# Row scores and causal mask of an attention step, written in squares of 32 output rows

## The chip, the core and the metric

The kernel runs on one core of a Trainium2 chip. The metric is the device time of one execution in microseconds (us), as the median of several runs. Before the change it is 2014.7 us, the median of 3 runs that lie between 2012.65 and 2017.67 us.

## What is computed

64 images of 3 x 224 x 224 are cut into 196 patches each and projected to 256 features; a bias and a position table are added, and 32 text rows are appended, so that a sequence has 228 rows. One transformer layer follows:

```python
h = _L0_tok_ref(x, W_embed, b_embed, pos_embed)
h = jnp.concatenate([h, txt], axis=1)                 # 64 x 228 x 256
h = h + attention(_layernorm(h), Wq, Wk, Wv, Wo, bo)   # 16 heads of 16, causal
h = h + ffn(_layernorm(h), w_up, w_down)               # ternary weights, 1024 wide, gelu
...
scores = jnp.einsum('bhqd,bhkd->bhqk', q, k) / jnp.sqrt(jnp.float32(hd))
scores = jnp.where(causal, -jnp.inf, scores)
probs = jax.nn.softmax(scores, axis=-1)
```

## The kernel before

Two sequences make a pair (32 pairs). A sequence is held as two blocks of R = 114 rows. The program is a software pipeline written out by hand: `step(t, hs)` has eight sections k = 0 to 7, and in step t it works on four pairs at once, pair t (patches, embedding, normalisation, queries and keys), pair t-1 (row scores and values), pair t-2 (column scores, softmax, weighted values) and pair t-3 (projection and feed-forward). There are 35 steps. The order of the work on each engine is the order of the calls in its own `step`; waits on semaphores tie the engines together.

The softmax needs the largest score of every query row. For that the scores are computed twice:

- **Row scores** (`scores_rows`, line 495): queries on the partitions, keys along the free axis. Section k takes one sequence of the pair and four heads. VectorE takes the maximum along the rows (`maxima_unit`, lines 951 and 952) and the maxima are folded into the queries. Only the maxima of these scores are used.
- **Column scores** (`scores_columns`, line 475): keys on the partitions. ScalarE takes their exponential (line 674), GpSimd zeroes what is above the diagonal (line 1155), and TensorE multiplies with the values (`weighted_values`, into the tile `pvps`).

In `scores_rows` four heads are worked on side by side. Head i has its queries and keys on the 32 partitions `quad(i)`, so that its matmul uses one strip of 32 rows of the array, and it writes to a PSUM bank of its own, `score[:, i]`. For query block qb = 0 a head has one matmul with 114 output rows and 114 keys, for qb = 1 one with 114 output rows and 228 keys. Both operands are float32; such a matmul stands in the trace as two loads and two matmuls, called its two passes below. Then the causal mask is added, in bfloat16: `cmask` holds a large negative number above a diagonal, `idm` a 32 x 32 identity with zeros to its left and right. For j = 0 to 3 a matmul per head adds the mask to output rows 32j and up of both diagonal blocks. All of its 114 output rows are written; those that aren't of piece j get zeros from the zeros around the identity. One call of `scores_rows` thus has 8 float32 matmuls (16 in the trace) and 16 bfloat16 ones, and it is made 8 times for each pair, 256 times in all. It is called the **row unit** below. Its last matmul signals VectorE.

Around a row unit in section k stand matmuls that use the whole array and write to the tile `dense` (embedding, up and down projection and so on), then the column scores (the tile `score`, `km` as the stationary operand), then the weighted values. A column unit has 8 float32 matmuls, and so has a unit of the weighted values; its squares are strips of 32 output rows over all rows of the array.

All matmuls pass through one helper, line 324, so that the trace's groups on it are told apart by their tiles: `score<-km,qm` are row scores, `score<-cmask,idm` the mask, `score<-qm,km` column scores, `pvps<-pr,vp` weighted values.

Of the kernel before, what the change touches and what calls it, by code (L numbers as in the profile page):

```python
# [39 lines left out]
S = NPATCH + TXT  # L40
R = S // 2
# [11 lines left out]
SW = S + R  # L53
# [22 lines left out]
def build(nc, x, txt, w_embed, b_embed, pos, wqkvo, bo, w_upT, w_downT, out):  # L76
    with ExitStack() as ctx:
        def sb(name, shape, dt):
            return ctx.enter_context(nc.sbuf_tensor(name, shape, dt))

        def sem(name):
            return ctx.enter_context(nc.semaphore(name))
# [3 lines left out]
        idm = sb("idm", [128, R + 96], BF16)  # L86
        cmask = sb("cmask", [128, R + 96], BF16)
# [21 lines left out]
        qm = sb("qm", [128, 2, 2, 2, T2], F32)  # L109
        km = sb("km", [128, 2, 2, 2, T2], F32)  # L110
# [42 lines left out]
        score = ctx.enter_context(nc.psum_tensor("score", [128, 4, 512], F32))  # L153
# [19 lines left out]
        p = {n: sem("p_" + n) for n in ["mask", "gl", "bo", "rstd1", "pw2", "acc", "ss", "w"]}  # L173
# [5 lines left out]
        def count(per, pair, k):  # L179


            return (min(pair, NPAIR - 1) if isinstance(pair, int) else pair) * per + k
# [34 lines left out]
        def score_emptied(t, k, columns):  # L217

            m, back = 2 * k + (1 if columns else 0) - 1, 0
            while back < 3:  # L220
                if m < 0:
                    m, back = m + 16, back + 1
                if m % 2 == 1:
                    pair, q = columns_of(t - back, m // 2)
                    if live(pair):
                        return a["exp"], count(8, pair, q + 1)
                elif live(t - back - 1):
                    return v["max"], count(8, t - back - 1, m // 2 + 1)
                m -= 1
            return a["w"], 1  # L230
# [91 lines left out]
        def _(eng):  # L322
            def mm(*args, **kw):
                return nc.tensor.matmul(*args, **kw)  # L324
# [147 lines left out]
            def quad(i):  # L472
                return slice(32 * i, 32 * i + 32)
# [21 lines left out]
            def scores_rows(t, u, k):  # L495

                b, r = divmod(k, 4)
                m, par = divmod(r, 2)
                if b == 0:
                    eng.wait_ge(a["q"], count(4, t - 1, 2 * m + par + 1))  # L500
                    if par == 0:
                        eng.wait_ge(v["km"], count(2, t - 1, m + 1))
                    else:
                        eng.wait_ge(a["km"], count(2, t - 1, m + 1))

                eng.wait_ge(*score_emptied(t, k, False))
                for qb in range(2):
                    for i in range(4):
                        mm(score[0:R, i, qb * R:qb * S + R], qm[quad(i), par, 1 - u, m, b * S + qb * R:b * S + qb * R + R],
                           km[quad(i), 1 - u, m, par, b * S:b * S + R + qb * R], start=True, stop=False,  # L510
                           skip_group_check=True)
                for j in range(4):
                    for i in range(4):
                        o = score[0:R, i, 0:SW].rearrange("p (x w) -> p x w", w=R)[:, 0:3:2, 32 * j:R]
                        above = cmask[quad(i), 96:96 + R - 32 * j].rearrange("p (o w) -> p o w", o=1)
                        last = mm(o, idm[quad(i), 96 - 32 * j:96 - 32 * j + R], above.broadcast_to([32, 2, R - 32 * j]),
                                  start=False, stop=True, skip_group_check=True)
                last.then_inc(pe["s"], 1)

# [35 lines left out]
            def step(t, hs):  # L555
                u = hs % 2
                A, Bm, Cc, Dd = live(t), live(t - 1), live(t - 2), live(t - 3)
                for k in range(8):
                    if Bm:
                        scores_rows(t, u, k)  # L560
# [695 lines left out]
```

## Time and profile before

| | |
|---|---|
| median of 3 runs | 2014.7 us |
| the profiled execution's own time | 2019.13 us |
| its span, first to last instruction | 2017.4 us |
| TensorE busy | 1927.3 us (96%), 25090 matmuls |
| VectorE busy | 1465.9 us (73%) |
| ScalarE busy | 1312.9 us (65%) |
| GpSimd busy | 892.5 us (44%) |
| granted TensorE clock, mean | 0.978 of full speed |

The times of a single instruction in the trace overlap with those of the next ones, since matmuls are pipelined: a matmul's record reaches from its issue to a modelled end. What a unit costs is read from where the next unit starts. In the timeline, rows of equal operation and tiles are merged into one, with the first one's shapes and the number of them; a narrow window lists those alone that are under way in it.

### The profile page before, as it was taken

The page shows a single profiled execution, that of the slowest core. Times are in us where ns is not written, and L with a number is a line of the kernel's source. Part 1 is how long each engine was busy: PE and PEld are TensorE (multiplying, and loading weights), DVE is VectorE, ACT ScalarE, POOL GpSimd, SP SyncE. Part 2 cuts the span into 40 slices and gives each one's busy share as a digit, 9 for nine tenths or more (in the row PEclk, how much of TensorE's full clock was granted, in tenths as well). Part 3 has the DMA queues.
Part 4 walks back from the last instruction along what each step waited for, and adds up shares of the span by engine and source line. Part 5 has one row for each costly group of instructions (what it writes and reads, how often), then busy time and mean ns, then how long its engine had stood idle before and what let it go on. Part 6 is the DMA issues. An engine that isn't in the chain of part 4 may idle for free.

```text
span 2017.4 us, 59822 instructions
## 1 busy us (share of the span) xinstructions
PE 1927.3 (96%) x25090; PEld 1574.9 (78%) x25090; DVE 1465.9 (73%) x2717; ACT 1312.9 (65%) x1986; POOL 892.5 (44%) x1067
## 2 busy tenths in 40 slices
PE   4779999999999999999999999999999999999975
PEld 3668888888888888788888888888888888888754
DVE  3667778777777777777777777777777778777753
ACT  3347766666776676767667677666667766667652
POOL 1124444444444544444454444444454445444543
PEclk8789999999999999999999999999999999999987
DMA  5011111111111101111111111111111111010000
GB/s 149 15 46 41 50 55 50 35 45 44 53 50 55 50 27 53 41 55 50 53 47 31 47 49 51 54 50 35 45 45 52 50 55 50 30 51 17 30 29 24
DMA packets 66116, 93.72 MB, mean 46 GB/s; under 512 B 10082, under 2 KB 59718, under 8 KB 65592
## 3 DMA queue, kind: packets, MB, share of 16 engines
q1 hardware_dynamic: 65848, 89.90, 15.6%
q8 instruction: 199, 3.26, 0.7%
q14 instruction: 69, 0.57, 0.1%
HBM read 45.03 MB, written 14.94 MB: 30 GB/s over the span
## 4 chain that ended last, share of the span: by engine, by line
PE 90%; ACT 3%; DVE 3%; issue 2%; POOL 1%; DMA 1%; SPq 0%; DVEq 0%; POOLq 0%; ACTq 0%
PE dense L324 50%; PE score L324 21%; PE pvps L324 9%; PE dense L342 4%; PE dense L381 3%; ACT qm L699 2%; PE dense L552 2%; PE dense L370 1%; POOL acc L1174 1%; DMA borow<-bo 1%; DVE mx L952 1%; ACT pr L674 0%; DVE st L936 0%; DVE mx L951 0%; ACT xn L723 0%
## 5 line engine op out<-in xcount | busy, mean ns | idle before, releaser
L1155 POOL TENSOR_SCALAR_AFFINE_SELECT pr<-pr 114x456 f32<-114x456 f32 x512 | 310.8, 631 | 853.2 <-ACT pr L674 853.2
L674 ACT ACTIVATE pr<-score 114x1368 f32<-114x1368 f32 x256 | 335.6, 1311 | 301.3 <-PE score L324 301.0
L951 DVE TENSOR_REDUCE mx<-score 114x4 f32<-114x456 f32 x256 | 161.1, 629 | 260.3 <-PE score L324 259.7
L952 DVE TENSOR_REDUCE mx<-score 114x4 f32<-114x912 f32 x256 | 281.0, 1098 | 0.0
L324 PE MATMUL dense<-wdn,g 128*114 128x256 bf16 x1024 | 243.4, 283 | 2.0 <-ACT g L683 1.2
L324 PE MATMUL score<-qm,km 32*114 32x228 f32 (+1 forms) x4096 | 221.8, 331 | 18.7 <-DVE mx L952 15.4
L324 PE MATMUL dense<-wdn,gl 128*114 128x256 bf16 x1024 | 236.6, 276 | 0.0
L1174 POOL TENSOR_TENSOR acc<-acc,sq 128x456 f32<-128x456 f32 x192 | 222.4, 1158 | 19.0 <-POOL acc L1174 0.4
L324 PEld LDWEIGHTS score<-qm,km 32*114 32x114 f32 x4096 | 176.0, 175 | 69.4 <-issue 40.5
L324 PE MATMUL score<-km,qm 32*114 32x114 f32 (+1 forms) x4096 | 221.8, 331 | 7.5 <-ACT pr L674 6.7
L324 PE MATMUL pvps<-pr,vp 114*32 114x228 f32 (+1 forms) x4096 | 205.2, 318 | 1.0 <-ACT raw L741 0.6
L908 DVE RECIPROCAL rs<-rs 128x228 f32<-128x228 f32 x128 | 200.5, 1566 | 5.5 <-DMA cx<-raw 5.5
L324 PEld LDWEIGHTS score<-km,qm 32*114 32x114 f32 x4096 | 127.1, 175 | 60.1 <-issue 37.9
L324 PEld LDWEIGHTS pvps<-pr,vp 114*32 114x32 f32 x4096 | 108.5, 110 | 68.9 <-POOL pr L1155 10.9
L683 ACT ACTIVATE g<-dense 128x456 f32<-128x456 f32 x256 | 135.1, 553 | 29.9 <-PE dense L324 29.4
L324 PEld LDWEIGHTS dense<-wdn,g 128*114 128x114 bf16 x1024 | 137.3, 134 | 19.8 <-issue 16.3
L324 PE MATMUL dense<-pT_hi,we_hi 128*128 128x392 f32 x384 | 142.3, 371 | 3.8 <-DVE pT_lo L898 2.2
L691 ACT ACTIVATE sq<-g 128x456 f32<-128x456 f32 x256 | 142.2, 580 | 1.4 <-POOL acc L1174 1.4
L324 PE MATMUL dense<-xT_hi,wup 128*128 128x456 f16 x512 | 142.8, 361 | 0.1
L716 ACT ACTIVATE vp<-dense 114x512 f32<-114x512 f32 x64 | 41.1, 642 | 156.2 <-PE dense L324 156.2
L324 PE MATMUL dense<-xT_lo,wup 128*128 128x456 f16 x512 | 141.7, 359 | 0.0
L324 PEld LDWEIGHTS dense<-wdn,gl 128*114 128x114 f16 x1024 | 136.2, 133 | 0.0
(125 smaller groups left out, 4402.5 us busy)
## 6 DMA issues: line engine op xcount, KB each, us to landing
pix<-x SPq DMA_DIRECT2D x64, 588.0 KB
rs<-raw SPq DMA_DIRECT2D x256, 57.0 KB, 2.0
cx<-raw SPq DMA_DIRECT2D x256, 57.0 KB, 2.0
out<-h SPq DMA_DIRECT2D x64, 228.0 KB
h<-txt SPq DMA_DIRECT2D x32, 64.0 KB, 7.1
km<-wqkvo SPq DMA_DIRECT2D x1, 1024.0 KB, 13.7
h<-w_upT SPq DMA_DIRECT2D x1, 1024.0 KB, 14.1
km<-w_embed SPq DMA_DIRECT2D x1, 768.0 KB, 6.6
```

The costliest lines, as they stand in the source:

```text
L324: return nc.tensor.matmul(*args, **kw)
L342: last = nc.tensor.transpose(ps[:, i * PROWS:(i + 1) * PROWS], patches[:, ph, n], ident[0:PROWS, 0:PROWS])
L381: last = nc.tensor.transpose(ps[:, col(blk, b):col(blk, b) + R], src[:, c0:c0 + 128], ident[0:R, 0:R])
L674: act(pr[q % 2][:], score[0:R, :, 0:SW], ACT.Exp, scale=float(HD) ** -0.5).then_inc(a["exp"], 1)
L683: act(g[:, m], bank_of("up", m)[:, 0:T2], ACT.Gelu).then_inc(a["gelu"], 1)
L691: act(sq[:, m % 4], g[:, m], ACT.Square).then_inc(a["sq"], 1)
L716: act(dst, bank_of("v", k)[0:R, 0:2 * D].rearrange("p (e c) -> p e c", c=HD), ACT.Copy).then_inc(a["v0"], 1)
L908: nc.vector.reciprocal(rs[:, k % 2], rs[:, k % 2]).then_inc(v["rs"], 1)
L951: nc.vector.tensor_reduce(mx[:, m, 0, x:128:32], score[0:R, :, 0:R], AX.X, ALU.max)
L952: nc.vector.tensor_reduce(mx[:, m, 1, x:128:32], score[0:R, :, R:SW], AX.X, ALU.max).then_inc(v["max"], 1)
L1155: nc.gpsimd.affine_select(out=blocks, in_=blocks, compare_op=ALU.is_ge, fill=0.0, base=0, pattern=[[0, 4], [1, R]], channel_multiplier=-1) ...
L1174: tt(acc[:], sq[:, 0] if m == 1 else acc[:], sq[:, m % 4], ALU.add).then_inc(p["acc"], 1)
```

## The change

Each float32 matmul of 114 output rows becomes four of 32, 32, 32 and 18 output rows, with the same moving operand. Each mask matmul writes the 32 (or 18) output rows that belong to its piece j, with the identity alone as the stationary operand. Queries of rows 32j and up are loaded into rows of strip i and columns 32j to 32j+31 of the array: a square (i, j). A row unit has 32 float32 matmuls (64 in the trace) and 16 bfloat16 ones then. Nothing else is changed, on no other engine.

```diff
                 eng.wait_ge(*score_emptied(t, k, False))
                 for qb in range(2):
+                    for j in range(4):
+                        lo, hi = 32 * j, min(32 * j + 32, R)
+                        for i in range(4):
+                            mm(score[lo:hi, i, qb * R:qb * S + R],
+                               qm[quad(i), par, 1 - u, m, b * S + qb * R + lo:b * S + qb * R + hi],
+                               km[quad(i), 1 - u, m, par, b * S:b * S + R + qb * R], start=True, stop=False,
+                               skip_group_check=True)
+                for j in range(4):
+                    lo, hi = 32 * j, min(32 * j + 32, R)
                     for i in range(4):
-                        mm(score[0:R, i, qb * R:qb * S + R], qm[quad(i), par, 1 - u, m, b * S + qb * R:b * S + qb * R + R],
-                           km[quad(i), 1 - u, m, par, b * S:b * S + R + qb * R], start=True, stop=False,
-                           skip_group_check=True)
-                for j in range(4):
-                    for i in range(4):
-                        o = score[0:R, i, 0:SW].rearrange("p (x w) -> p x w", w=R)[:, 0:3:2, 32 * j:R]
-                        above = cmask[quad(i), 96:96 + R - 32 * j].rearrange("p (o w) -> p o w", o=1)
-                        last = mm(o, idm[quad(i), 96 - 32 * j:96 - 32 * j + R], above.broadcast_to([32, 2, R - 32 * j]),
+                        o = score[lo:hi, i, 0:SW].rearrange("p (x w) -> p x w", w=R)[:, 0:3:2, lo:R]
+                        above = cmask[quad(i), 96:96 + R - lo].rearrange("p (o w) -> p o w", o=1)
+                        last = mm(o, idm[quad(i), 96:96 + hi - lo], above.broadcast_to([32, 2, R - lo]),
                                   start=False, stop=True, skip_group_check=True)
                 last.then_inc(pe["s"], 1)
```

On TensorE, in section 3 between two groups of the up projection, the row unit stood in the program before as follows (output shapes are written behind the tiles; a float32 matmul is one row here).

```order
L324 MATMUL dense<-xT_hi,wup 128x456 x2
L324 MATMUL dense<-xT_lo,wup 128x456 x2
L324 MATMUL score<-km,qm 114x114 x4
L324 MATMUL score<-km,qm 114x228 x4
L324 MATMUL score<-cmask,idm 114x2x114 x4
L324 MATMUL score<-cmask,idm 114x2x82 x4
L324 MATMUL score<-cmask,idm 114x2x50 x4
L324 MATMUL score<-cmask,idm 114x2x18 x4
L324 MATMUL dense<-xT_hi,wup 128x456 x2
L324 MATMUL dense<-xT_lo,wup 128x456 x2
```

The same place in the changed program:

```order
L324 MATMUL dense<-xT_hi,wup 128x456 x2
L324 MATMUL dense<-xT_lo,wup 128x456 x2
L324 MATMUL score<-km,qm 32x114 x12
L324 MATMUL score<-km,qm 18x114 x4
L324 MATMUL score<-km,qm 32x228 x12
L324 MATMUL score<-km,qm 18x228 x4
L324 MATMUL score<-cmask,idm 32x2x114 x4
L324 MATMUL score<-cmask,idm 32x2x82 x4
L324 MATMUL score<-cmask,idm 32x2x50 x4
L324 MATMUL score<-cmask,idm 18x2x18 x4
L324 MATMUL dense<-xT_hi,wup 128x456 x2
L324 MATMUL dense<-xT_lo,wup 128x456 x2
```

The unit keeps its place between the same neighbours; 8 float32 matmuls became 32, and the 16 of the mask stayed 16 with fewer output rows.

## Rows read from the trace of the kernel before

**Rows 1.** The page: busy time by engine, and the chain that ended last.

```profile
PE 1927.3 (96%) x25090; PEld 1574.9 (78%) x25090; DVE 1465.9 (73%) x2717; ACT 1312.9 (65%) x1986; POOL 892.5 (44%) x1067
...
PE 90%; ACT 3%; DVE 3%; issue 2%; POOL 1%; DMA 1%; SPq 0%; DVEq 0%; POOLq 0%; ACTq 0%
```

**Rows 2.** Busy time by stretch: window, us, busy us of each engine, granted clock.

```profile
1000.00:1057.60 57.60, 57.52 (x773) 46.84 (x772) 43.41 (x82) 40.86 (x62) 26.19 (x33) 1.00 0.14 40
...
0.00:120.00 120.00, 78.39 (x828) 67.01 (x828) 62.87 (x105) 48.28 (x67) 15.93 (x31) 0.87 0.30 83
120.00:1900.00 1780.00, 1764.77 (x23423) 1443.81 (x23424) 1344.29 (x2506) 1213.64 (x1840) 825.40 (x983) 1.00 0.16 45
1900.00:2017.00 117.00, 84.11 (x841) 64.10 (x838) 58.74 (x108) 51.02 (x81) 51.16 (x53) 0.82 0.08 25
```

**Rows 3.** Timeline, TensorE: start us, us, operation and tiles, count; a row unit.

```profile
1011.50 0.55 PE L324 MATMUL dense<-xT_lo,wup 128*128 128x456 f16 x2
1011.97 0.86 PE L324 MATMUL score<-km,qm 32*114 32x114 f32 x16
1012.65 0.42 PE L324 MATMUL score<-cmask,idm 32*114 32x228 bf16 x16
1013.00 0.56 PE L324 MATMUL dense<-xT_hi,wup 128*128 128x456 f16 x2
```

**Rows 4.** The same unit's matmuls through narrow windows, one after the other.

```profile
1011.97 0.37 PE L324 MATMUL score<-km,qm 32*114 32x114 f32 x4
...
1012.16 0.47 PE L324 MATMUL score<-km,qm 32*114 32x114 f32 x8
...
1012.26 0.57 PE L324 MATMUL score<-km,qm 32*114 32x228 f32 x8
...
1012.46 0.37 PE L324 MATMUL score<-km,qm 32*114 32x228 f32 x4
1012.65 0.28 PE L324 MATMUL score<-cmask,idm 32*114 32x228 bf16 x4
...
1012.75 0.32 PE L324 MATMUL score<-cmask,idm 32*114 32x164 bf16 x12
...
1012.82 0.25 PE L324 MATMUL score<-cmask,idm 32*114 32x100 bf16 x8
```

**Rows 5.** The same unit's second loads, through a narrow window.

```profile
1012.07 0.29 PEld L324 LDWEIGHTS score<-km,qm 32*114 32x114 f32 x8
```

**Rows 6.** Narrow windows on the column unit's end and the weighted values behind it.

```profile
1008.63 0.28 PE L324 MATMUL score<-qm,km 32*114 32x114 f32 x4
1008.84 0.40 PE L324 MATMUL pvps<-pr,vp 114*32 114x228 f32 x4
...
1009.05 0.48 PE L324 MATMUL pvps<-pr,vp 114*32 114x228 f32 x8
```

**Rows 7.** A row unit of section 5, and where TensorE's sequencer was then.

```profile
1028.20 0.86 PE L324 MATMUL score<-km,qm 32*114 32x114 f32 x16
1028.87 0.42 PE L324 MATMUL score<-cmask,idm 32*114 32x228 bf16 x16
1029.22 0.32 PE L324 MATMUL dense<-wdn,g 128*114 128x256 bf16 x1
...
1028.20 0.47 PE L324 MATMUL score<-km,qm 32*114 32x114 f32 x8
...
L462 PEldq EVENT_SEMAPHORE  x1: 51/51/51, 1028.4 to 1028.4; - x1
```

**Rows 8.** Row-score matmuls in the first 120 us, and after 1900 us.

```profile
L324 PE MATMUL score<-km,qm x176: 258/351/587, 50.7 to 116.0; 32*114 32x114 f32 x88, 32*114 32x228 f32 x88
...
L324 PE MATMUL score<-km,qm x64: 258/350/353, 1906.2 to 1925.5; 32*114 32x114 f32 x32, 32*114 32x228 f32 x32
```

**Rows 9.** Timeline, VectorE, behind the unit of rows 7; then the next column unit.

```profile
1029.34 0.63 DVE L951 TENSOR_REDUCE mx<-score 114x4 f32<-114x456 f32 x1
1029.89 1.10 DVE L952 TENSOR_REDUCE mx<-score 114x4 f32<-114x912 f32 x1
...
1031.13 0.46 PE L324 MATMUL score<-qm,km 32*114 32x228 f32 x4
```

**Rows 10.** The page's DMA queues: the queue that brings instructions.

```profile
q8 instruction: 199, 3.26, 0.7%
```

## The prediction

> **What bounds the kernel now.** I start with the page. TensorE is busy for 96% of the span and the chain that ended last runs through it for 90% [rows 1]. Busy shares are means, so the busy time by stretch comes next: in a steady step of 57.6 us TensorE is busy 57.52 us, VectorE 43.41, ScalarE 40.86 and GpSimd 26.19, at the full granted clock [rows 2]. From 120 to 1900 us TensorE is free for 15 us in all; only the filling and the draining of the pipeline leave it idle [rows 2]. In the steady part a microsecond taken off TensorE's work is a microsecond off the span, until another engine fills the step; the next one, VectorE, has 14 us of room.
>
> Since the records of matmuls overlap, the price of a row unit is read from the timeline, from its first matmul to the first of its successor: 1011.97 to 1013.00, which is 1.03 us [rows 3], and 1028.20 to 1029.22, 1.02 us, in another section [rows 7]. There are 256 units. The first 120 us hold 176/16 = 11 of them and the time after 1900 us 64/16 = 4 [rows 8], which leaves 241 in the stretch where TensorE sets the pace.
>
> **What a unit's time is made of.** Narrow windows on one unit give its parts [rows 4]. The four heads' first passes start together: four records of 348 ns take 0.37 us from the first's start to the last's end, so the four starts lie within 0.02 us, 7 ns apart. The second loads begin at 1012.07 [rows 5], so that a first load of 114 columns takes 0.10 us; the second passes start at 1012.16, after 0.09 us more of streaming. The passes over 228 keys start at 1012.26 and 1012.46, the mask at 1012.65. A strip thus streams for 0.09 + 0.10 + 0.20 + 0.19 = 0.58 us behind one load of 0.10 us that nothing covers; later loads lie under running passes. The four mask rounds start at 1012.65, 1012.75, 1012.82 and some 0.04 us later, and the successor at 1013.00: 0.35 us, of which 0.11 us is the gap that any such unit has behind its last matmul (the column unit's last passes of 0.10 us start at 1008.63 and the next unit at 1008.84 [rows 6]). Check: 0.10 + 0.58 + 0.10 + 0.07 + 0.04 + 0.02 + 0.11 = 1.02 us.
>
> **The change, part by part.**
>
> *Score matmuls, 8 to 32 of them (16 to 64 passes).* The moving columns for each square are the same as for a strip now, so if all sixteen squares stream side by side, each still needs 0.58 us. That four column groups can stream different operands at once is shown by the weighted values: their first passes start at 1008.84 and the second at 1009.05, for four groups together [rows 6]. The same rows give the load of 32 columns: 0.21 us less the 0.19 us of a 228-wide pass is 0.02 to 0.03 us. The uncovered first load thus shrinks by 0.07 us.
>
> *Mask, 16 matmuls as before.* Now a strip takes the four pieces one after the other, 0.10 + 0.07 + 0.04 + 0.02 us. Then square (i, j) takes piece j alone: the longest chain loses the 0.13 us of pieces 1 to 3. The loads of 114 columns behind them, hidden now, become loads of 32.
>
> *Starting sixteen squares in place of four.* This is what the change pays with. The trace shows a start each 7 ns in a group of four; what it costs for sixteen, no row shows. One bound: 7 ns buys both passes of a square, since both stand in the list before the next head's. Then the last square starts 15 x 7 = 0.10 us behind the first. The other bound: 7 ns is the price of one load-and-pass pair. Then it starts 0.20 us behind. The last square has j = 3 and the shortest mask piece, so the unit is 0.10 + 0.03 + 0.58 + 0.02 + 0.11 = 0.84 us by the first bound and 0.94 us by the second. Of squares with j = 0 the last starts 0.02 to 0.04 us late, and ends with 0.84 to 0.86 us. I take 0.93 us: with sixteen squares the second passes fall due while first ones still go out, so they do take slots, as the second bound has it, though not each.
>
> The page "TensorE: Matmul & The Clock Gate" of the Trainium skill, section "Part 3: Packing small matmuls — row/col tiling", gives about 4 ns per further tile for a packed group. By that price the last square would start 0.06 us late and the unit would take 0.80 to 0.82 us, the kernel some 52 us less; my sum doesn't use it, since it is for single-pass matmuls.
>
> *More instructions.* 24 more float32 matmuls per unit are 96 more records, 256 x 96 = 24,576 in all. The instruction queue brings 3.26 MB in 199 packets for 0.7% of the DMA engines' time [rows 10]; half as much again stays hidden beside DMA engines that are 16% busy [rows 2].
>
> *What waits for the unit.* VectorE's two maxima end 1.65 us after they start (1029.34 to 1030.99) and TensorE's next column unit starts at 1031.13 [rows 9]. Both ends hang on the row unit's end, and the work between is unchanged, so no wait appears. A step would be 0.8 us shorter, 56.8 us, with VectorE at 43.4.
>
> **The sum.** 1.03 - 0.93 = 0.10 us for 241 units is 24 us; the 15 at the ends I count as nothing, since TensorE waits for others there. The profiled execution took 2019.13 us (span 2017.4), 4.4 us above the median of 2014.7. So 1995 us for that execution, and **1991 us** for the median. With 0.84 us for the unit and all 256 counted it would be 2014.7 - 49 = 1966 us.
>
> **Rivals.** About 0.3%, 6 us, is what a measurement of this kernel can tell from no change; that is 0.025 us a unit.
>
> *A: the engine cannot feed the squares (slower).* A unit has 80 load-and-pass pairs then, for 32 now. One per 11 ns is the point where nothing is gained: 80 x 0.011 + 0.03 + 0.11 = 1.02 us. At 13 ns, twice the measured spacing, it is 1.18 us and the kernel 0.15 x 241 = 36 us longer, 2051 us. For it: the trace never shows more than 32 pairs per 1.03 us over a whole unit, and 7 ns only over four in a row. Against it: at 1028.4 the sequencer already stood at the wait of line 462, which comes behind the whole unit, while eight of 32 matmuls had started [rows 7]. It had handed over all 64 instructions in 0.2 us or earlier, so the handing over isn't slow.
>
> *B: squares of one strip go in order (slower).* The passes of a square depend on each other. If a strip of the array takes its work in program order, square j+1 can't start before square j's second pass has. Second passes would begin at 0.12, 0.22, 0.32 and 0.42 us, then 0.20 us apart up to 1.22; the unit ends at 1.42 + 0.02 + 0.11 = 1.55 us, and the kernel takes 0.52 x 241 = 125 us more, 2140 us. The same page and section of the Trainium skill speak for it: loads are said to overlap with running matmuls only where the row group differs, and matmuls to start in program order. Against it: the four second passes start behind all four first ones, at 1012.16 against 1011.97, though each head's two stand together, and the weighted values do the same with four column groups that share all rows [rows 4, 6]. So order isn't kept between strips, nor between column groups; for both at once no row speaks.
>
> *C: the look-ahead is too short (about no change).* To have sixteen squares under way the engine must look over 64 instructions at least. Rows 7 show it with eight of 32 matmuls started and the rest handed over, some 44 instructions. If it holds little more, eleven or twelve squares run at once, the later ones start with the second passes of the first, some 0.1 us late, and again in the wider passes: the unit is 0.95 to 1.05 us, the kernel 1996 to 2020 us. The half of this below 1.00 us still counts as faster.
>
> **How the numbers follow.** The forecast, 0.84 to 0.98 us for the unit, has a chance of 0.66: each of its parts (the streaming, the 32-column load, starts 7 ns apart, passes that overtake) is seen in a row, though not together. C has 0.15, of which 0.03 is faster, 0.10 within 0.3% and 0.02 slower. A has 0.10, B 0.09. That gives 0.69 faster, 0.10 same, 0.21 slower. The range reaches from 1964 us (all squares in 0.10 us, with the scatter of the runs) to 2035 us, which holds C and the milder half of A; B and the rest of A, 0.14, are left out above, and about 0.04 below.
>
> **What would show it.** In the changed profile: a row unit's first matmul to its successor's in 0.93 us; sixteen first passes within 0.10 to 0.20 us, before or among the second ones; the mask's matmuls within some 0.2 us; loads of row scores at about the weighted values' duration; a steady step of 56.8 us with TensorE still busy throughout. It would be wrong if starts in a unit come 11 ns or more apart per pair (A), if a second group of four first passes waits for the second passes of the group before (B), or if starts come in two waves with a pause after some twelve squares (C).

## The result and the profile after

The changed kernel takes 2094.2 us, the median of 4 runs between 2083.6 and 2101.2. The kernel before, run beside it, takes 2015.4 us. The ratio is 1.039 with a 95% interval of 1.0354 to 1.0425: slower by 79 us, where 24 us less were forecast. The profiled execution took 2089.4 us, with a span of 2087.6 us, 70.2 us more than the span before.

The page of the changed kernel; these are the lines of [rows 1] and [rows 10], and the granted clock in 40 slices.

```profile
PE 1982.7 (95%) x37378; PEld 1580.5 (76%) x37378; DVE 1466.9 (70%) x2717; ACT 1313.0 (63%) x1986; POOL 891.2 (43%) x1067
...
PEclk9899999999999999999999999999999999999988
...
q8 instruction: 295, 4.83, 1.0%
...
PE 90%; ACT 3%; DVE 3%; issue 2%; POOL 1%; DMA 1%; SPq 0%; DVEq 0%; POOLq 0%; ACTq 0%
```

TensorE is the bound as before, and the other engines' busy times are those of before. The added time is TensorE's own. Two stretches by window, as in [rows 2] (a steady step now, and the middle of the span):

```profile
1070.00:1129.10 59.10, 59.01 (x1147) 47.28 (x1145) 43.35 (x83) 39.55 (x61) 26.75 (x33) 1.00 0.17 48
...
120.00:1900.00 1780.00, 1753.25 (x33578) 1400.24 (x33579) 1292.73 (x2410) 1166.83 (x1767) 791.40 (x944) 0.99 0.16 45
```

A step took 57.6 us and takes 59.1 us, at the full clock and with TensorE busy throughout. In the middle 1780 us TensorE is now idle for 27 us, for 15 before. So there are two places to look: inside the row unit, and in the new idle time.

**Inside a row unit.** The timeline of TensorE, as in [rows 3]. Rows of one operation are merged, with the shape of the first.

```profile
1003.85 0.27 PE L324 MATMUL dense<-wdn,gl 128*114 128x256 bf16 x1
1004.06 1.03 PE L324 MATMUL score<-km,qm 32*32 32x114 f32 x53
1004.75 0.26 PE L324 MATMUL score<-cmask,idm 32*32 32x228 bf16 x1
1004.75 0.51 PE L324 MATMUL score<-km,qm 32*32 32x228 f32 x11
1004.93 0.41 PE L324 MATMUL score<-cmask,idm 32*32 32x228 bf16 x15
1005.27 0.22 PE L324 MATMUL dense<-onesb,acc 128*114 128x1 bf16 x1
```

From the unit's first matmul to its successor's are 1.21 us, for 1.03. The median over the 256 units is 1.213 us, for 1.024; the column units (0.78 us) and the weighted values (0.72 us) are as they were. The difference of 0.19 us times 256 is 48.4 us of the 70.2.

Narrow windows on the same unit, one after the other, as in [rows 4] (at 1004.10, 1004.15, 1004.28, 1004.55 and 1004.65 us):

```profile
1004.06 0.33 PE L324 MATMUL score<-km,qm 32*32 32x114 f32 x9
...
1004.06 0.37 PE L324 MATMUL score<-km,qm 32*32 32x114 f32 x16
...
1004.06 0.47 PE L324 MATMUL score<-km,qm 32*32 32x114 f32 x32
...
1004.36 0.56 PE L324 MATMUL score<-km,qm 32*32 32x228 f32 x8
...
1004.36 0.65 PE L324 MATMUL score<-km,qm 32*32 32x228 f32 x14
```

Between the third and the fourth, from 1004.40 to 1004.45 us, the view by tile tells the shapes apart (count, then durations in ns, starts, shapes):

```profile
L324 PE MATMUL score<-km,qm x23: 256/256/348, 1004.1 to 1004.4; 32*32 32x114 f32 x14, 32*18 32x114 f32 x8, 32*32 32x228 f32 x1
```

And this is all that the array loads at 1004.45:

```profile
1004.37 0.10 PEld L324 LDWEIGHTS score<-km,qm 32*32 32x32 f32 x1
```

- Nine first passes of query block 0 are under way at 1004.11 and sixteen at 1004.15; all 32 passes of the block have started by 1004.28. Seven starts in 0.05 us are 7 ns each, and the last square starts 0.10 us behind the first: the forecast's first bound to the letter.
- Then it stops. At 1004.40 to 1004.45 a single pass over 228 keys is under way, and one weight load. From 1004.27 to 1004.46 us the array begins this pass and this load and nothing else, though all waits of the unit on semaphores stand ahead of its first matmul.
- Then starts come evenly, but slower: 8 passes under way at 1004.55 and 14 at 1004.65, none having ended between. Six starts in 0.10 us are 17 ns each, so about 4 ns for each of a square's four instructions (two loads and two passes).
- The mask's first matmul starts at 1004.75. By the single starts in the trace its second and third follow at 1004.93 and 1004.94, and the other thirteen only from 1005.06 on. Second score passes still start in between, but the mask is held up twice.

**Between the units.** TensorE's waits with no cause in the profile (us in total, times, longest); before, these summed to 0.9 us, all on `dense`:

```profile
PE score L324 <- issue: 5.1, 3, 2.2
PE dense L324 <- issue: 4.6, 3, 3.2
PE pvps L324 <- issue: 3.3, 3, 1.2
PE dense L342 <- issue: 2.7, 2, 2.4
```

15.7 us in 11 waits. The longest in the timeline:

```profile
1029.15 0.28 PE L324 MATMUL dense<-wa_lo,aT_hi 128*114 128x256 f32 x1
1032.60 0.37 PE L324 MATMUL dense<-wa_hi,aT_hi 128*114 128x256 f32 x1 [3.16 <-issue]
```

The windows on it and behind it (columns as in [rows 2]):

```profile
1029.00:1033.00 4.00, 0.84 (x7) 0.73 (x5) 1.53 (x2) 0.00 (x0) 0.29 (x1) 0.88 0.27 69
1033.00:1037.00 4.00, 4.00 (x36) 3.44 (x39) 2.06 (x7) 2.31 (x5) 0.00 (x0) 0.50 0.02 4
```

The DMA queues from 1027 to 1033 us (packets, MB, share of the 16 engines' time):

```profile
q1 hardware_dynamic: 199, 0.72, 46.4%
q8 instruction: 1, 0.02, 1.3%
```

TensorE stands for 3.2 us between two matmuls of one chain, and the profile shows nothing that it waits for. One packet of the instruction queue falls into the stretch, while the DMA engines are 46% busy with other packets, mostly of 7168 bytes, which are pixels. By the single packets of the trace, pixel loads run in the 3 us ahead of every such stop of 0.4 us or more in the steady part, ten in all. They also show that TensorE goes on 1.2 to 1.5 us behind the end of a 16.4 KB packet of the instruction queue, in all ten; the queue brings one such packet in 7 us on average. Behind the stop the granted clock is 0.50, TensorE's lower level of 1.2 GHz, in the whole window of 4 us. The `dense` matmuls of 256 columns start 0.21 us apart there (1032.77 and 1032.98), for 0.12 us ahead of the stop.

### The profile page after: what moved, and what is told of

It reads as the page before. It is cut to its first block, busy times and chain, and to the rows that moved or that the text cites. A ratio compares the mean times of both kernels' runs of the same rounds, so it can differ in the third digit from the quotient of the medians.

```text
span 2087.6 us, 84398 instructions
## 1 busy us (share of the span) xinstructions
PE 1982.7 (95%) x37378; PEld 1580.5 (76%) x37378; DVE 1466.9 (70%) x2717; ACT 1313.0 (63%) x1986; POOL 891.2 (43%) x1067
## 3 DMA queue, kind: packets, MB, share of 16 engines
q8 instruction: 295, 4.83, 1.0%
## 4 chain that ended last, share of the span: by engine, by line
PE 90%; ACT 3%; DVE 3%; issue 2%; POOL 1%; DMA 1%; SPq 0%; DVEq 0%; POOLq 0%; ACTq 0%
PE dense L324 49%; PE score L324 23%; PE pvps L324 9%; PE dense L342 4%; PE dense L381 3%; ACT qm L703 2%; PE dense L556 2%; PE dense L370 1%; POOL acc L1178 1%; DMA borow<-bo 1%; DVE mx L956 1%; ACT pr L678 1%; DVE mx L955 0%; DVE st L940 0%; ACT xn L727 0%
## 5 line engine op out<-in xcount | busy, mean ns | idle before, releaser
L324 PE MATMUL score<-km,qm 32*32 32x114 f32 (+3 forms) x16384 | 310.9, 317 | 7.6 <-ACT pr L678 6.7
L324 PEld LDWEIGHTS score<-km,qm 32*32 32x32 f32 (+1 forms) x16384 | 173.5, 100 | 81.7 <-issue 38.5
L324 PE MATMUL score<-cmask,idm 32*32 32x228 bf16 (+3 forms) x4096 | 153.0, 222 | 0.0
```

## What the experiments had to tell apart

Two theories stand for the row unit.

**Q, the places.** TensorE holds 64 instructions, loads and passes alike. A place comes free in program order, when its instruction has completed, and is filled again some 25 to 30 ns later, one instruction per 4.15 ns (by the single starts, the squares of block 1 come 16.6 ns apart). The first 16 squares are 64 instructions, so they find places. Instruction 4 of the unit is the first square's second pass. It starts only at 1004.18, since it needs the square's first, and its record ends at 1004.43; until then no place beyond it comes free, even if others behind it are done. The second square of block 1 starts at 1004.47, right behind. The mask fits in the same way. Instruction 68, the second pass of block 1's first square, ends at 1004.90, and instruction 132, the mask's second matmul, starts at 1004.93; instruction 72 ends at 1005.03, and 136, the mask's fourth, starts at 1005.06. Each time the one that starts stands 64 places behind the one that ends. The unit before has exactly 64 instructions, mask included, so by Q none of them has to wait for another to complete.

**S, the strip in order.** It is rival B of the forecast: within one strip of 32 array rows work goes in program order.

For the idle time stands theory **F, the fetch**: instructions come in packets of 4.83 MB / 295 = 16.4 KB, the same size as before (3.26 / 199), there are half as many more, and a packet that falls due while pixels are loaded comes late.

A replay of one unit by Q's rules, with the durations of the records, is an estimate, not a measurement. It gives 1.00 us for the kernel before (measured 1.02) and 1.22 us for the change (1.21). With 48 places it would give 1.60 us for the change. With 128 places it would give 0.93 us; no run can show that, and the figure depends on how fast waiting squares are taken to start. What tests Q are the unit times that it named before the runs below.

## Experiments

**Halves.** Pieces of 64 and 50 output rows, scores and mask: 96 instructions a unit instead of 160.

```diff
-                    for j in range(4):
-                        lo, hi = 32 * j, min(32 * j + 32, R)
+                    for j in range(2):
+                        lo, hi = 64 * j, min(64 * j + 64, R)
...
-                    lo, hi = 32 * j, min(32 * j + 32, R)
+                    top, lo = 64 * (j // 2), 32 * j
+                    hi = min(top + 64, R)
...
-                        last = mm(o, idm[quad(i), 96:96 + hi - lo], above.broadcast_to([32, 2, R - lo]),
+                        last = mm(o, idm[quad(i), 96 - (lo - top):96 - lo + hi], above.broadcast_to([32, 2, R - lo]),
```

> Scores and mask in pieces of 64 output rows (64 and 50) in place of 32: eight pieces, 64 score instructions and 32 of the mask per row unit, so 96 in place of 160 (64 before the change). Theory Q (TensorE can hold 64 instructions, a place comes free in program order when an instruction has completed, and later ones follow at about 4 ns each): the 32 passes of the narrow matmuls fit the queue whole, so the unit takes 0.90 us (0.10 us less than strips, for two mask pieces in a row in place of four), the kernel 1985 to 1998 us. Theory S (pieces of one strip of rows hold each other up, whatever the queue): two pieces cost a part of what four cost, 1.05 to 1.15 us, the kernel 2020 to 2045 us.

Measured: 1992.9 us, ratio 0.9904 [0.9874, 0.9935], faster than before. The unit in the timeline:

```profile
1007.71 0.82 PE L324 MATMUL score<-km,qm 32*64 32x114 f32 x32
1008.35 0.35 PE L324 MATMUL score<-cmask,idm 32*64 32x228 bf16 x16
1008.62 1.09 PE L370 MATMUL dense<-ident,hT 128*114 128x128 f32 x8
```

It takes 0.91 us, where Q had named 0.90. So the idea of the change is sound, and its grain was too fine. In section 1 alone the unit still takes 1.02 us (the median of its 29 steady units, for 0.91 in each other section); why is seen in the trimmed halves below.

**Mask alone in squares.** The scores stay strips, the mask is as in the change. The lines below are against the kernel before.

```diff
-                        o = score[0:R, i, 0:SW].rearrange("p (x w) -> p x w", w=R)[:, 0:3:2, 32 * j:R]
+                        o = score[lo:hi, i, 0:SW].rearrange("p (x w) -> p x w", w=R)[:, 0:3:2, lo:R]
...
-                        last = mm(o, idm[quad(i), 96 - 32 * j:96 - 32 * j + R], above.broadcast_to([32, 2, R - 32 * j]),
+                        last = mm(o, idm[quad(i), 96:96 + hi - lo], above.broadcast_to([32, 2, R - lo]),
```

> Scores in strips of 114 output rows as before the change, the mask alone in squares; 64 instructions as before. Both theories: the longest mask chain in a square is one piece of 0.10 us in place of 0.23. If the array can pass from strips to squares without a pause the unit takes 0.80 to 0.90 us and the kernel 1975 to 1990 us; if it must first drain (0.1 us), as between any two units now, the gain is used up, 1.00 to 1.04 us and 2008 to 2018 us.

Measured: 2012.9 us, ratio 0.9988 [0.9971, 1.0005], no difference. The unit:

```profile
1001.49 0.86 PE L324 MATMUL score<-km,qm 32*114 32x114 f32 x16
1002.27 0.28 PE L324 MATMUL score<-cmask,idm 32*32 32x228 bf16 x16
1002.48 0.45 PE L324 MATMUL dense<-pT_hi,we_hi 128*128 128x392 f32 x1
```

A narrow window on its last score passes:

```profile
1001.97 0.37 PE L324 MATMUL score<-km,qm 32*114 32x228 f32 x4
```

The unit takes 0.99 us. From the mask's first matmul to the successor are 0.21 us, for 0.35 us before, so the mask chain did shrink by 0.14 us, as forecast. But the mask starts 0.78 us into the unit instead of 0.68. The last score passes stream until 1001.97 + 0.19 = 1002.16, and the mask waits 0.11 us more: between strips and squares the array runs empty. Some 0.03 us a unit are left, 8 us in 256 units, of which the ratio shows 2 us, within the noise. In the change itself both are squares, and this cost doesn't arise: there the mask's first matmul starts at 1004.75, as soon as its square's last score pass has streamed (from 1004.55, for 0.19 us).

**Squares head by head.** The same 160 instructions; the loops over heads and pieces are exchanged, so that the four squares of a strip follow each other.

```diff
-                    for j in range(4):
-                        lo, hi = 32 * j, min(32 * j + 32, R)
-                        for i in range(4):
+                    for i in range(4):
+                        for j in range(4):
+                            lo, hi = 32 * j, min(32 * j + 32, R)
```

> The changed kernel with its score squares issued strip by strip (heads outside, pieces inside). Theory Q: the order in which the sixteen squares stand doesn't matter while all fit the queue, unit 1.21 us, the kernel within 1% of the changed one (2080 to 2105 us). Theory S (a strip takes its squares in order): a strip's squares now stand next to each other and block the strips behind, the unit takes 1.5 us or more, the kernel over 2150 us.

Measured: 2097.4 us, ratio 1.0422 [1.0371, 1.0473], the change's own time within the intervals. The unit is the change's:

```profile
1005.54 1.03 PE L324 MATMUL score<-km,qm 32*32 32x114 f32 x53
1006.24 0.25 PE L324 MATMUL score<-cmask,idm 32*32 32x228 bf16 x1
```

The mask starts 0.70 us into the unit, the change's 0.69, and the median unit is 1.215 us. If a strip took its squares in order, this order would be the worst. S falls.

**Squares without the mask.** The change, with the 16 mask matmuls left out (so the maxima include keys behind the query; 128 instructions a unit).

```diff
-                for j in range(4):
-                    lo, hi = 32 * j, min(32 * j + 32, R)
-                    for i in range(4):
...
-                        last = mm(o, idm[quad(i), 96:96 + hi - lo], above.broadcast_to([32, 2, R - lo]),
-                                  start=False, stop=True, skip_group_check=True)
```

> The changed kernel without the causal mask matmuls (left out: the mask of the row scores). 128 instructions per unit. Theory Q: the scores alone take about 1.13 us to the next unit, since the wide passes wait for places in the queue; the last 32 instructions cost only 0.09 us. Kernel about 2065 us. If instead the mask's squares were what is slow, the unit would fall to about 0.8 us and the kernel to 1965 us.

Measured: 2058.0 us, ratio 1.0226 [1.0176, 1.0277].

```profile
1000.60 1.20 PE L324 MATMUL score<-km,qm 32*32 32x114 f32 x64
1001.73 0.21 PE L324 MATMUL dense<-onesb,acc 128*114 128x1 bf16 x1
```

1.13 us for the scores alone, as Q had named it, is more than the whole unit before. The loss lies in the score squares; the mask in squares adds only 0.08 us.

**Square by square.** The same 160 instructions once more, with both query blocks of a square one behind the other.

```diff
-                for qb in range(2):
-                    for j in range(4):
-                        lo, hi = 32 * j, min(32 * j + 32, R)
-                        for i in range(4):
+                for j in range(4):
+                    lo, hi = 32 * j, min(32 * j + 32, R)
+                    for i in range(4):
+                        for qb in range(2):
```

> The changed kernel with the same 160 instructions, ordered square by square: for each square the 114-wide and then the 228-wide matmul, then the next square. Theory Q: 64 places hold eight squares only, and a place comes free in program order, so the second eight wait for the first ones' wide passes: unit 1.75 us by a model of the queue, the kernel 2190 to 2240 us. If only the number of instructions or of squares counted, the time would stay at that of the changed kernel, 2085 to 2105 us.

Measured: 2224.0 us, ratio 1.1045 [1.0991, 1.1099]. The unit is 1.76 us long, where Q had named 1.75:

```profile
1002.15 1.37 PE L324 MATMUL score<-km,qm 32*32 32x114 f32 x48
...
1003.91 0.32 PE L324 MATMUL dense<-wdn,g 128*114 128x256 bf16 x1
```

With eight dependent instructions per square in a row, 64 places hold eight squares, not sixteen. Count and kinds of instructions are those of the change, and a fixed price per instruction would give the change's 1.21 us. What differs is how long the oldest of the 64 take. This run, with the one head by head, speaks for Q against both S and a fixed price.

**Squares with few pixels, and strips with few pixels.** For the idle time between the units. In both kernels the pixels of all pairs but the first are one source row instead of 84. So the output is of other images; the instructions are the same.

```diff
-                sp.dma_start(pix[:, half], xp[bass.ds(pair * PROWS, PROWS), half]).then_inc(s_pix[ph], 16)
+                n = PROWS if pair == 0 else 1
+                sp.dma_start(pix[0:n, half], xp[bass.ds(5 * PROWS, n), half]).then_inc(s_pix[ph], 16)
```

> The changed kernel, but only the first pair's pixels are loaded; for each later pair one row of the 84 is (left out: the images of the other pairs). Theory F (the pauses of 1.3 to 3.4 us in which TensorE waits for nothing recorded are waits for a page of instructions whose fetch stands behind the pixel load on the DMA engines): the pauses between 150 and 1800 us are gone, TensorE's idle time put down to issue falls from 15.7 to under 3 us, the kernel 2068 to 2080 us. Rival: the sequencer outruns its instruction fetch whatever the other transfers do, since there are half as many instructions again: pauses and time stay as they are, 2085 to 2100 us.

> The kernel before the change with the same pixels left out. Theory F: it has no pauses of over 1 us in the steady part to lose, so it stays within 4 us of the kernel before, 2010 to 2016 us; the difference to the squares with few pixels is then the row units alone, 0.19 us x 256 = 48 us plus at most 10. If pixel loads slow the kernel in another way than through the instruction fetch, this one gains as much as the squares do.

Measured: the change with few pixels 2065.3 us, ratio 1.0255 [1.0222, 1.0287]; the kernel before with few pixels 2013.4 us, ratio 0.9993 [0.9977, 1.0009]. The whole list of waits without a cause is one line in the former:

```profile
PE dense L325 <- issue: 0.9, 2, 0.7
```

The change with few pixels lies 3 us below the range that F had named, the kernel before inside it. The unit stays at 1.21 us. The same omission is worth nothing in the kernel before and some 27 us (1.039 less 1.0255, of 2015; by the two intervals give or take 10) in the change. So the long stops need both the added instructions and the pixel loads, and each ends at much the same distance behind an instruction packet: F holds. In which way the loads hold a packet up isn't shown. Of these 27 us the waits themselves are 15.7 - 0.9 = 14.8. The rest fits the low clock behind them. Between 150 and 1890 us the trace of the change has five stretches at a granted clock of 0.50, each beginning within 2 us of a stop's end, 27 us together; the trace with few pixels has none. Work at half the clock takes twice as long, which makes some 13 us by estimate. What is left of the loss, 2065 - 2013 = 52 us, is the squares: 256 x 0.19 us is 48.4. So the 79 us split into about 52 for the places (give or take 7) and 27 for the fetch (give or take 10).

**Halves, trimmed.** A version meant to beat both. The upper halves compute only the keys up to row 63 of their block; the rest is behind the diagonal, where the mask adds to what the bank holds from earlier. The lines below show what differs from the halves.

```diff
-                            mm(score[lo:hi, i, qb * R:qb * S + R],
+                            mm(score[lo:hi, i, qb * R:qb * S + hi],
...
-                               km[quad(i), 1 - u, m, par, b * S:b * S + R + qb * R], start=True, stop=False,
+                               km[quad(i), 1 - u, m, par, b * S:b * S + hi + qb * R], start=True, stop=False,
```

> Pieces of 64 output rows, and the upper piece (rows 0 to 63) is computed only up to key 63 of its diagonal block (for the second query block up to key 177), since the mask covers the rest for these rows. Same 96 instructions. Theory Q: with all passes in the queue the unit is set by the longest chain in the array; the upper piece's chain loses (50 + 50) x 4 / 2.4 ns = 0.17 us, the lower piece's stays, which has the short mask pieces: unit 0.83 us, 0.08 us less than without the trimming, the kernel 1968 to 1980 us. If instructions set the time, it stays at 1990 to 1996 us.

Measured: 1987.4 us, ratio 0.9854 [0.9809, 0.99]: faster than all before it, but short of the expected time by 7 us or more, though the median unit is 0.816 us. Compared unit by unit with the kernel before, some 200 of the 233 units between 120 and 1850 us fell by 0.2 us. The 29 of section 1 didn't: 27 of them stayed at 1.02 to 1.05 us, two at 1.56 us. One of them:

```profile
1509.23 0.82 PE L324 MATMUL score<-km,qm 32*64 32x64 f32 x31
...
1510.25 0.38 PE L324 MATMUL dense<-wa_hi,aT_hi 128*114 128x256 f32 x1
```

Its successor's first load, with its wait:

```profile
1510.25 0.17 PEld L324 LDWEIGHTS dense<-wa_hi,aT_hi 128*114 128x114 f32 x1 [0.25 <-DVE pT_lo L903]
```

VectorE's work beside it:

```profile
1509.36 0.27 DVE L1062 TENSOR_SCALAR ve<-mv 114x4 f32<-114x4 f32 x1
1509.54 0.15 DVE L1063 COPY ve<-mv 114x4 f32<-114x4 f32 x1
1509.61 1.08 DVE L903 TENSOR_TENSOR pT_lo<-dense,pT_hi 128x420 fp32r<-128x420 f32 x2
```

The matmuls behind the unit need a bank that VectorE empties with `pT_lo`. TensorE now arrives 0.25 us early and waits. TensorE's loads that waited for `pT_lo` between 120 and 1900 us (us in total, times, longest), in the kernel before, the halves, the trimmed halves and the next run:

```profile
PEld dense L324 <- DVE pT_lo L898: 6.2, 31, 0.6
PEld dense L324 <- DVE pT_lo L903: 13.0, 55, 0.8
PEld dense L324 <- DVE pT_lo L903: 12.8, 54, 0.8
PEld dense L324 <- DVE pT_lo L903: 4.6, 26, 0.2
```

So the untrimmed halves had this wait already: it is why their unit stayed at 1.02 us in section 1. It explains some 27 x 0.2 = 5 us of what is missing. Stops without a cause, 7.7 us here, are a further part.

**The same with VectorE reordered.** On VectorE, two small operations that stood ahead of `pT_lo` go behind it; on TensorE nothing changes.

```diff
+                    if A and k == 0:
+                        pixels_lo(t, 0)
+                        pixels_lo(t, 1)
+                        pixels_lo(t, 2)
+                    if Dd and k == 0:
                         eng.wait_ge(v["mv2"], count(4, t - 3, 4))
...
-                    if A and k == 0:
-                        pixels_lo(t, 0)
-                        pixels_lo(t, 1)
-                        pixels_lo(t, 2)
```

> Pieces of 64 rows with the trimmed keys as in the run before, and one change on VectorE: in section 0 the three low parts of the pixels (pT_lo) stand ahead of the two small operations on the variances instead of behind them. Reading of the run before: 206 of 233 steady row units took 0.82 us instead of 1.02, but the 27 of section 1 still took 1.02, since TensorE then reached the values' matmuls 0.25 us before VectorE had emptied their bank with the last pT_lo but two. If that is the wait, those units fall to 0.82 to 0.90 us and the kernel by 27 x 0.12 to 0.2 = 3 to 6 us: 1981 to 1985 us, the wait for pT_lo gone from TensorE's list. If something else holds them (the array, the queue of 64), the units of section 1 stay at 1.02 us and the time at 1987. If the small operations were needed early by GpSimd, a wait for pw or rm appears and the time rises above 1988.

Measured: **1979.8 us**, ratio 0.9823 [0.9794, 0.9852], the lowest of all versions and 1 us below the range expected. Its interval overlaps that of the trimmed halves, so the step between the two isn't shown by the times. A unit of section 1:

```profile
1496.07 0.82 PE L324 MATMUL score<-km,qm 32*64 32x64 f32 x31
...
1496.89 0.38 PE L324 MATMUL dense<-wa_hi,aT_hi 128*114 128x256 f32 x1
```

It takes 0.82 us, as does the median unit of section 1. No matmul of the steady part waits for `pT_lo` any more, and the loads wait half as often. The span of the profiled execution is 1979.0 us, for 1986.3.

**The same with few pixels.** As above, one source row.

> The run before it in this call, and the pixels of all pairs but the first are one source row instead of 84 (image data left out, the output is of other images). Theory F, that instruction pages wait behind pixel loads: TensorE's issue stalls (7.7 us in the variant before, 5 of them of 0.8 to 2.4 us) go, and with them the slow clock behind each: 8 to 12 us less than the run beside it, 1970 to 1977 us. Rival, that stalls come from the number of instructions alone: no difference beyond 3 us.

Measured: 1970.7 us, ratio 0.9786 [0.9756, 0.9816], against 0.9823 beside it. The list of TensorE's waits has no line without a cause left; in the version beside it there are 8.7 us of them in five waits, each ending 1.3 to 1.5 us behind an instruction packet. The spans differ by 12.8 us, the medians by 9.2, and the intervals of the ratios overlap, so the size isn't sharp. The disappearance of the waits is. A kernel with 96 instructions a unit still pays about 10 us for late instruction packets, by these two runs. How to avoid it without leaving pixels out (smaller or earlier pixel loads) wasn't tried.

## Why the prediction was wrong

**The bound, the streaming, the overlap: right.** TensorE sets the pace, and a step changes by 8 units' worth: 59.1 - 57.6 = 1.5 us, which is 8 x 0.19. Sixteen squares run side by side, second passes overtake, and sixteen starts cost 7 ns each. That strips and column groups overlap at once was argued from two separate rows [rows 4, 6]; the squares and the halves show it. The mask chain shrank by 0.14 us, forecast at 0.13, where it could be seen alone.

**"Starting sixteen squares in place of four": the step that failed.** It priced a start and nothing else: 0.93 us were forecast for the unit and 1.21 measured. The starts themselves came as its first bound had them, so the error isn't in that term but in a missing one, the wait for a place among the 64 that TensorE holds: 0.28 us. It takes the place of a gain of 0.10 us a unit and makes a loss of 0.19. It came about in two ways.

- Rival C had the mechanism, and mis-sized it. It took the look-ahead from [rows 7] as "some 44 instructions" or little more and asked only how many squares are under way at once. It gave 0.95 to 1.05 us and called that about no change. The hold is 64 instructions, enough for sixteen squares of one block. What costs is that places come free in program order, so the first square's second pass, whose record ends 0.38 us into the unit, keeps sixty others closed. [Rows 7] bore on it: at 0.2 us into the old unit everything had been handed over, and that unit has just 64 instructions, mask included. The row could show no larger hold, and the new unit has 160. With that count C deserved more than 0.15, and a higher price.
- Rival A was dismissed with "the handing over isn't slow". That holds while places are free. Once they aren't, the engine lives on the refill, 4.15 ns per instruction or 8.3 ns per load-and-pass pair. This is below the 11 ns at which A would have decided, so A as written fell. But refilled at that rate the sixteen squares of block 1, 64 instructions, take 0.27 us to come in, behind a stop of 0.2 us.

**Rival B fell**, with the run head by head. The rule of the Trainium skill that spoke for it ("TensorE: Matmul & The Clock Gate", "Part 3: Packing small matmuls — row/col tiling"), that loads overlap with running matmuls only where the row group differs and that matmuls start strictly in order, disagrees with the narrow windows above: sixteen first passes on four strips within 0.10 us, with second passes behind them that stand ahead in the list. The same page of the Trainium skill gives TensorE a queue of 64 instructions with partial reordering. The runs here agree with the number: in each pair above, the start stands 64 places behind the end. The page says nothing on when a place comes free.

**"More instructions": wrong too**, by about 27 us, where the forecast had nothing. The step looked at the instruction queue's share of the DMA engines' time (0.7%) and their mean load (16%). The mean says nothing of a single packet that TensorE can't go on without: within [rows 2]'s 16% there are stretches where pixel loads take far more, 46% in the one shown, and behind or within ten of these TensorE stood still. The Trainium skill ("Runtime: NRT & Kernel Launch", "Instruction fetch mechanics") holds that fetching is hidden by the pace at which instructions are issued, some 20 cycles each. Here they enter at 4 ns each, and the waits with and without pixels show that it isn't always hidden.

**"What waits for the unit": right** for the change, where the unit grew. It wouldn't have held for a unit as short as the forecast's: at 0.91 and 0.82 us a wait for `pT_lo` appears in section 1, which "no wait appears" had ruled out.

## What to carry to other kernels

Before small matmuls are cut further, count the instructions (a load and a matmul per pass, two passes per float32 matmul) from the next one to the oldest still unfinished: past 64, in these runs, nothing new is taken in until the oldest is done. So put independent work between the dependent passes of one square; the same 160 instructions took 1.21 us so and 1.76 us square by square. And choose the largest piece that still overlaps; here 64 rows won where 32 lost. And more instructions have a price of their own where bulk loads share the DMA engines with the instruction queue: look for waits without a cause, and for the clock behind them.

## What was unexpected of the hardware

- The hold of 64 instructions, freed in order: a stop of 0.2 us inside a unit whose operands are all there, and 1.76 us for a unit of the same instructions in another order.
- Between strips of 114 output rows and squares of 32 the array ran empty for 0.11 us, which ate most of the mask's gain of 0.14 us.
- Late instruction packets: stops of up to 3.2 us, all but gone without the pixel loads, each ending 1.2 to 1.5 us behind a packet, and over 4 us at a granted clock of 0.50 behind the longest.
